# The inverse root of a group norm: twelve VectorE operations or one GpSimd power

## The reference

```python
a4 = att.reshape(b, l, H, S)                      # H = 32 heads, S = 8 channels
m = jnp.mean(a4, axis=-1, keepdims=True)
var = jnp.mean((a4 - m) ** 2, axis=-1, keepdims=True)
att = ((a4 - m) * jax.lax.rsqrt(var + EPS)).reshape(b, l, E) * gn_w + gn_b
x = x + att * g @ Wo.T
```

## Time and profile before

| | us | share of the span |
|---|---|---|
| median of three runs | 694.92 | |
| the profiled execution, first to last instruction | 694.0 | 100% |
| PE busy | 645.3 | 93% |
| PE weight loads | 561.6 | 81% |
| DVE busy | 598.2 | 86% |
| ACT busy | 571.7 | 82% |
| POOL busy | 311.6 | 45% |
| PE's share of the chain that ended last | | 80% |

### The profile page before, as it was taken

One profiled execution on the slowest core, in us unless ns is written; L12 is line 12 of the kernel. 1 busy time (PEld: TensorE's weight loads), 2 busy tenths in 40 slices (PEclk: granted clock), 3 DMA queues, 4 the chain that ended last, 5 costly groups with the idle time before them and its releaser, 6 DMA issues.

```text
span 694.0 us, 17297 instructions
## 1 busy us (share of the span) xinstructions
PE 645.3 (93%) x5877; PEld 561.6 (81%) x5877; DVE 598.2 (86%) x1430; ACT 571.7 (82%) x2071; POOL 311.6 (45%) x440
## 2 busy tenths in 40 slices
PE   6878998999999999999999999999999989898776
PEld 5666787888989888988989888989888877687555
DVE  3598588999999999999999999999999987968274
ACT  1568899899999999999999999999999987664513
POOL 1154252646464554636364646454554624432120
PEclk9999999999999999999999999999999999999799
DMA  8920031221305050504122231305050503120200
GB/s 306 325 70 9 2 104 36 70 70 58 88 9 138 1 146 1 145 2 122 25 85 62 67 81 53 93 4 144 1 146 1 146 0 108 31 70 0 69 9 8
DMA packets 53725, 50.44 MB, mean 73 GB/s; under 512 B 6030, under 2 KB 48902, under 8 KB 53254
## 3 DMA queue, kind: packets, MB, share of 16 engines
q1 hardware_dynamic: 53638, 49.34, 24.7%
HBM read 28.62 MB, written 3.93 MB: 47 GB/s over the span
## 4 chain that ended last, share of the span: by engine, by line
PE 80%; DVE 8%; ACT 7%; issue 3%; POOL 1%; DMA 0%; SPq 0%; DVEq 0%; ACTq 0%; POOLq 0%
PE PS_B L552 16%; PE PS_T L654 9%; PE PS_B L694 8%; PE PS_S L552 7%; PE PS_D L559 5%; PE PS_S L625 4%; PE PS_T L662 4%; PE PS_S L559 4%; PE PS_T L559 4%; ACT SC L1291 3%; PE PS_D L800 2%; PE PS_B L703 2%; PE PS_D L552 2%; ACT PT L1301 2%; PE PS_T L545 2%
## 5 line engine op out<-in xcount | busy, mean ns | idle before, releaser
L1291 ACT ACTIVATE SC<-SC,NMX 128x128 f32<-128x128 f32 x512 | 200.0, 398 | 0.2
L1291 ACT ACTIVATION_READ_ACCUMULATOR SC<-SC,NMX 128x1 f32 x512 | 101.0, 197 | 0.0
L654 PE MATMUL PS_T<-CST,SC 128*128 128x128 f32 x512 | 81.3, 281 | 7.7 <-ACT PT L1301 3.6
L976 DVE TENSOR_REDUCE NMX<-SC 128x4 f32<-128x512 f32 x128 | 85.2, 676 | 0.4 <-POOL SC L1499 0.3
L1301 ACT ACTIVATE PT<-PS_T 128x512 f32<-128x512 f32 x120 | 70.8, 590 | 12.7 <-PE PS_T L654 12.7
L654 PEld LDWEIGHTS PS_T<-CST,SC 128*128 128x128 f32 x512 | 56.4, 141 | 26.1 <-ACT PT L1301 12.7
L1057 DVE TENSOR_TENSOR_SCAN SS<-W,AJ 128x1024 f32<-128x1024 f32 x32 | 73.2, 2288 | 0.2
L552 PE MATMUL PS_B<-MX,W 128*128 128x128 f32 x512 | 64.2, 280 | 4.7 <-ACT KR L1350 4.7
L552 PEld LDWEIGHTS PS_B<-MX,W 128*128 128x128 f32 x512 | 61.3, 196 | 4.9 <-ACT KR L1350 4.9
L1499 POOL TENSOR_TENSOR SC<-SC,MADD 128x512 f32<-128x512 f32 x48 | 59.9, 1276 | 6.5 <-DVE SC L956 6.5
L552 PE MATMUL PS_B<-B_LT,W 128*128 128x128 f32 x512 | 61.1, 278 | 1.0 <-ACT B_LT L1231 0.9
(11 more groups left out here) (231 smaller groups left out, 1595.0 us busy)
## 6 DMA issues: line engine op xcount, KB each, us to landing
W<-EW SPq DMA_DIRECT2D x32, 512.0 KB, 4.1
V<-values_by_head SPq DMA_DIRECT2D x28, 512.0 KB, 5.4
W<-in_weights SPq DMA_DIRECT2D x1, 4160.0 KB, 21.0
ENC<-in_enc SPq DMA_DIRECT2D x16, 128.0 KB, 2.3
out<-X SPq DMA_DIRECT2D x16, 128.0 KB, 5.8
X<-in_x SPq DMA_DIRECT2D x1, 1920.0 KB, 15.7
values_by_head<-VC SPq DMA_DIRECT2D x14, 128.0 KB, 1.8
W<-in_weights SPq DMA_DIRECT2D x1, 1280.0 KB, 8.5
```

The lines of the kernel that those rows point to most:

```text
L654: last = pe.transpose(PS_T[:, j * T:(j + 1) * T], SC[:, nr(b, a) % 2, g, j, :], ident)
L976: dve.tensor_reduce(NMX[:, nr(b, a) % 2, GH * g:GH * g + GH], SC[:, nr(b, a) % 2, g], AX_X, ALU.max, negate=True)\
L1291: last = act.activation(SC[:, nr(b, a) % 2, g, j, :], SC[:, nr(b, a) % 2, g, j, :], ACT.Exp, bias=NMX[:, nr(b, a) % 2, h:h + 1], accum_out ...
```

## The change

For the first fourteen sequences the sum of squares goes to SBUF (`GT`) instead of PSUM, the twelve operations of `d_guess` and `d_newton` go away, and a new POOL piece `d_group_root` adds epsilon to the mean of the squares (128x32, into `GE`) and raises it to the power -0.5 (128x32, into the new tile `GI`, from which `d_norm` reads). It stands in `POOL_ORDER` between `a_root` 1 and `a_addmask` (0, 2). `d_spread` waits until POOL has read `GT` of the sequence before, the power until DVE has read `GI` of the sequence before, and `d_norm` for the power. The last two sequences keep PSUM, root and reciprocal. No transfer is added, removed or moved.

```diff
 DVE_ORDER = [
...
-    ("a_normal", 1, 2), ("d_spread", 0, 5), ("d_guess", 0, 5), ("a_mask", (0, 3), 1), ("d_guess", 1, 5),
-    ("d_guess", 2, 5), ("a_maxima", (0, 1), 1), ("d_newton", (0, 0), 5), ("d_newton", (0, 1), 5),
...
+    ("a_normal", 1, 2), ("d_spread", 0, 5), ("a_mask", (0, 3), 1), 
+    ("a_maxima", (0, 1), 1), 
+    ("a_stats", 0, 0),
+    ("a_moments", 0, 0), ("a_context", 1, 3),
+    ("a_maxima", (0, 2), 1), ("a_addmask", (0, 3), 1), ("a_key", 1, 2),
+    ("a_normal", 0, 0), ("d_inverse", 0, 5), ("d_norm", 0, 5), ("d_ruk", 0, 4), ("a_sum", 1, 3),
...
 POOL_ORDER = [
...
-    ("a_root", 1, 2), ("a_addmask", (0, 2), 1), ("a_addbias", 0, 1), ("a_root", 0, 0), ("a_addbias", 1, 2),
+    ("a_root", 1, 2), ("d_group_root", 0, 5), ("a_addmask", (0, 2), 1), ("a_addbias", 0, 1), ("a_root", 0, 0), ("a_addbias", 1, 2),
...
-            return dbank(b)[:, 512 - 2 * RH:512 - RH]
+            return dbank(b)[:, 512 - 2 * RH:512 - RH] if b >= B - LAST else GT
 
         def GY(b):
-            return dbank(b)[:, 512 - 3 * RH:512 - 2 * RH]
+            return dbank(b)[:, 512 - 3 * RH:512 - 2 * RH] if b >= B - LAST else GI
...
             def d_spread(b, _):
                 dve.wait_ge(d_sq, b + 1)
+                dve.wait_ge(d_geps, min(b, B - LAST))
                 dve.tensor_reduce(GV(b)[:, :], heads(OQ[:, :]), AX_X, ALU.add).then_inc(d_v, 1)
...
             def d_norm(b, _):
                 if b < B - LAST:
-                    dve.wait_ge(d_gr, 12 * b + 12)
+                    dve.wait_ge(d_gr, b + 1)
...
+            def d_group_root(b, _):
+                if b >= B - LAST:
+                    return
+                pool.wait_ge(d_v, b + 1)
+                pool.tensor_scalar(GE[:, :], GT[:, :], 1.0 / RS, EPS, ALU.mult, ALU.add).then_inc(d_geps, 1)
+                pool.wait_ge(d_geps, b + 1)
+                pool.wait_ge(d_n, b)
+                pool.tensor_tensor(GI[:, :], GE[:, :], CST[:, K_POW:K_POW + 1].to_broadcast([P, RH]), ALU.pow)\
+                    .then_inc(d_gr, 1)
```

More of the change, by code:

```diff
@@ L204, in build @@
         CV, OW = sb("CV", [C]), sb("OW", [RH])
-        GE, GT = sb("GE", [RH]), sb("GT", [RH])
+        GE, GT, GI = sb("GE", [RH]), sb("GT", [RH]), sb("GI", [RH])
         YT = sb("YT", [CT, T])
@@ L309, in build @@
         d_gr = sem("d_gr")
+        d_geps = sem("d_geps")
         d_gsd = sem("d_gsd")
@@ L1214, in _ @@
                            b_mixed, b_streams, b_gate, d_outer, d_scan, d_ruk, d_rstate, d_own, d_output, d_means,
-                           d_centre, d_spread, d_relu2, d_shift, d_final, d_guess, d_newton, d_inverse, d_norm, d_gated, d_sum, d_stats,
+                           d_centre, d_spread, d_relu2, d_shift, d_final, d_inverse, d_norm, d_gated, d_sum, d_stats,
                            d_moments, d_mixed, d_mixing)
@@ L1568, in _ @@
             pieces = named(a_root, b_shift, d_shift, d_final, a_addbias, a_addmask, b_root, b_addbias, b_addnorm,
-                           d_rstate, d_gates, d_root)
+                           d_rstate, d_group_root, d_gates, d_root)
             for i in range(B + LAG):
```

## The result

The changed kernel takes 1.071 times the time of the kernel before, with an interval of 1.066 to 1.076: slower, by some 49 us where 10 were forecast. Its comparable runs took 743.3 and 743.9 us at a mean granted clock of 0.977; two others, at 0.953 and 0.955, took 756 and 758 us and are not compared, which is why the median of all four, 750.1, lies between. The profiled execution took 743.3 us, 741.5 of them between its first and last instruction, against 694.0.

What follows compares the result with a forecast made beforehand. PE was taken as the limit, DVE's freed time as worth nothing; a 2.7 us power on POOL, 1.9 us of it hidden, costs twelve turns 9.6 us: 694.0 + 9.6 = 703.6, so 704 us, range 690 to 833.

Steps and rivals of the forecast that it cites:

- the price of X: Duration of POOL's new 128x32 power: 2.7 us, the geometric middle of 0.61 (paid once) and 12.0 (paid per column).
- the same sum: Twelve turns each lose the power's duration above 1.9 us, 9.6 us at 2.7; the last two sequences lose nothing.
- the likeliest case: The power outlasts the cover ahead of L998, lasting 1.9 to 6 us: 694 to 749 us, 704 as its time; 41%.
- The bound: PE limits the kernel: in a turn of 37.10 us it is busy for 36.98, DVE for 35.81.
- The slack: Up to 1.9 us of the power is hidden ahead of L998; beyond that, QT and PE's scores are delayed one for one.
- the addition that I left out: By the State Buffer rule L1148 would wait about 0.3 us for POOL's bias row: 3.4 us more, 707.
- The gain of the twelve operations: DVE gets back about 1.8 us in a turn, beside PE's work, so costed at nothing.
- Hidden: Rival: the power lasts at most 1.9 us, covered by the wait ahead of L998; 694 or 693 us; 22%.
- Faster: Rival: DVE's freed 1.8 us bring an ACT copy forward for PE, 7.3 us less, 687 us; 5%.
- Every column pays: Rival: each column of POOL's power costs 368 ns, power of 6 to 12 us; 749 to 833 us; 32%.
- loss of clock: With PE idling many microseconds, a lower granted clock costs 1.7 us in each of 14 turns, 24 us more, 857.

Runs made afterwards that it cites:

- e4: The changed kernel with POOL's second bias row moved behind the root of the b norm; 1.070 of the kernel before (1.067 to 1.073).
- e1: The changed kernel with POOL multiplying the 32 columns by the constant instead of raising them to the power; 1.0009 of the kernel before.
- e5: The changed kernel with the power on 8 of the 32 columns, the other 24 holding a constant; 1.0009 of the kernel before.
- e6: The changed kernel with POOL's mask addition ahead of the two new operations and both bias rows behind the d norm's root; 1.064 of the kernel before.

## Why the prediction was wrong

**The step that failed is the price of X.** I put the power at 2.7 us, the geometric middle of 0.61 and 12.0; it takes 5.43. With 5.43 the same sum gives 12 x 3.53 = 42.4 us, and 1.7 and 2.8 for the last two after their idle time: 741 us for a profiled execution that took 741.5. The mechanism was the one forecast, and the term was a factor of two too small. The time lies inside the range, and inside the likeliest case's own (694 to 749).

That the sum with 5.43 comes within a microsecond is partly luck. The first eleven turns with a power took 453.6 us where they had taken 410.1: 43.5 us more, where the sum has 38.8 (11 x 3.53). All that follows them lost 4.1 us, where the sum has 8.1. The two misses cancel.

What misled me in that step: I split 548 ns into 180 that POOL's ordinary operations pay once and 368 for the column, and took the rest as a guess between two ends. The four points show 390 ns paid once and 158 for a column, 74 times the 2.14 ns of an addition. A middle on a scale of factors was a choice without a row, and it drew the value towards the lower end. The bound itself held.

**The slack** was 1.9 us in the forecast and is 1.55. I lay the sum of squares of the changed kernel (379.47) on that of the profile before (355.29). Then the forecast with 5.43 us puts L910 at 364.49 and L998 at 365.48, and they came at 364.39 and 365.79. So the path was right up to L910, and what is missing lies behind it: that operation, now L911, takes 0.81 us and not 0.41. I had seen such a meeting only in a pair of L1193 beside a short POOL operation, found no hold-up there, and added nothing. The trace of the kernel before has one that I overlooked, the same line beside a mask addition of POOL:

```profile
93.82 1.27 POOL L1501 TENSOR_TENSOR SC<-SC,MADD 128x512 f32<-128x512 f32 x1
```

```profile
93.89 1.35 DVE L910 TENSOR_SCALAR A_N<-X,A_MV,A_RS 128x256 f32<-128x256 f32 x1 [0.73 <-POOL A_RS L1470]
```

The Trainium skill's rule (SBUF — State Buffer, "Who interferes with whom") was the better guide: VectorE and GpSimd share a pair of ports to SBUF, and whichever operation takes it first keeps it for its whole length while the other waits. The trace agrees: where L910 or L911 begins while POOL is in an addition on 256 or 512 columns, it ends 0.14 to 0.16 us after that addition, wherever it began (95.24 after 95.09 in the trace before, 389.38 after 389.23 in the changed kernel, 350.18 after 350.04 in e4). That page of the Trainium skill counts an operation of this kind (a tensor with scalars) among those that can use the shared ports.

The product by the root, L1148 (now L1121), is where I had expected it. In the turn shown it starts after the bias row has ended (389.30 after 389.23) and takes 0.41 us. But for the thirteenth sequence it runs beside the row, and takes 0.94:

```profile
630.88 0.73 POOL L1456 TENSOR_TENSOR X<-X,ROW 128x256 f32<-128x256 f32 x1
```

```profile
630.94 0.94 DVE L1121 TENSOR_TENSOR O<-O,GI 128x256 f32<-128x256 f32 x1 [2.37 <-POOL GI L1526]
```

In e4, with the row moved away, the same product takes 0.43. So the addition that I left out was due in one of fourteen places, 0.5 us in all.

**The gain of the twelve operations** was put at nothing, and e1 measures nothing (1.0009). DVE's busy time did not fall by 31 us, though. In e1 it is 574.3 us, 24 less than before: the operations overlap by their ends, so the 31 us that I got by adding them up was the wrong sum for a busy time; the 1.8 us that I had estimated for a turn, fourteen times, give 25. In the changed kernel it is 580.3, 6.0 more than in e1. L911 puts 4.4 us of that back (18.3 us in its group for A_N against 13.9 in e1) and L1121 0.4; the rest I did not trace.

**The rivals.** "Hidden" fell with the power's own row, 5.43 us against the 1.9 that it allowed; its mechanism holds where the power is short (e5: 1.65 us, 1.0009). "Faster" falls with e1. "Every column pays" was half right: every column does pay, but 158 ns and not 368. Its loss of clock I had put at 1.7 us in every turn; in the profiled run four of the first eleven turns have a granted clock of 0.96 instead of 1.00, and lost 3.9 to 4.5 us where the others lost 3.8 to 3.9.

## What to carry to other kernels

Price an operation that the trace shows on one column by measuring it on two widths before it is moved in bulk; a single point cannot tell what is paid once from what each column pays. An engine that is idle for half of the time is no free place for a long operation: what counts is the queue behind it, here three short POOL operations with DVE, and then PE, waiting for them, and a slack of about 1.6 us. And the work taken off an engine that the chain did not name gave nothing back.

## What the runs showed of the hardware

The fp32 power on POOL costs 0.39 us and 158 ns a column of 128 rows: 0.55, 1.65, 2.91 and 5.43 us for 1, 8, 16 and 32 columns. A product on 32 columns takes 0.24.

A DVE operation of two per-row scalars on 128x256 (L910, L911), begun while POOL had an addition on 256 or 512 columns under way, ended 0.14 to 0.16 us after that addition: according to when it began, it took for example 0.61, 0.81 or 1.35 us where it takes 0.41 alone.

A stall of PE by some 2 us inside a turn in which it otherwise works nearly without a break was followed, in some turns and not in others, by a stretch at the lower granted clock. In the changed kernel, the five microseconds after the stall in an early turn and the four at the same place in a later one (busy time by engine, then the granted clock):

```profile
223.00:228.00 5.00, 4.16 (x30) 3.61 (x30) 4.61 (x12) 1.61 (x5) 2.34 (x6) 0.66 0.90 225
388.00:392.00 4.00, 2.83 (x26) 2.15 (x30) 3.61 (x10) 1.65 (x5) 1.97 (x4) 1.00 1.00 258
```

0.66 is a stretch that lay mostly at 1.2 GHz, 1.00 one at 2.4 GHz. Which turns are struck differs between runs, and a shorter stall is not always the safer one: in the profiled runs PE waits less in e6 than in the changed kernel (1.8 us against 3.1 up to the scores), and nine of its first eleven turns were struck against four. What decides it stays open.
